# A fused attention and expert kernel: the three-part split of k and q made with TensorE subtractions, the routing work and the squares dealt out anew

## What is computed

```python
q = (x @ Wq.T + bq).reshape(B, L, 16, 8);  k, v likewise        # B = 8 sequences of L = 512 rows, 128 wide
p = einsum('blhd,dm->blhm', q, proj) / sqrt(8)                 # 128 angles for each row and head
q_prime = concat([cos(p), sin(p)]) / sqrt(128);  k_prime likewise
kv = einsum('blhm,blhd->bhmd', k_prime, v);  out = einsum('blhm,bhmd->blhd', q_prime, kv)
x = layernorm(x + out @ Wo.T + bo)
# a mixture of 8 experts (128 -> 512 -> 128, relu), the 2 with the largest logits of x @ Wr + br for each row
x = layernorm(x + sum over the two of weight * expert(x))
```

## Time and profile before

| | before |
|---|---|
| median of three runs | 553.1 us (549.98 to 554.34) |
| profiled execution, its own time | 551.36 us |
| its span, first to last instruction | 549.6 us |
| busy: TensorE matmul, VectorE, ScalarE, GpSimd | 88%, 78%, 69%, 75% |
| mean granted TensorE clock | 0.959 of full speed |

### The profile page before, as it was taken

How to read it: one execution, slowest core, us unless ns; L and a number is a source line. 1 busy time by engine, 2 the same in 40 slices (tenths; PEclk the granted TensorE clock), 3 DMA queues, 4 the chain that set the end, 5 groups by cost and what they waited for, 6 DMA issues and landing times.

```text
span 549.6 us, 13153 instructions
## 1 busy us (share of the span) xinstructions
PE 483.9 (88%) x4205; PEld 297.4 (54%) x4205; DVE 427.8 (78%) x907; ACT 381.0 (69%) x533; POOL 410.7 (75%) x474
## 2 busy tenths in 40 slices
PE   6698889999999999999999989689999679999914
PEld 3333344444444444444344444158999678999802
DVE  6769978988988988988988888568677475777654
ACT  2686669789789789789789689376555244565325
POOL 2279549879879889879879889857677656777645
PEclk9899989999999999999999999799999789999957
DMA  4675504705704705604605400032222123222174
GB/s 96 169 228 160 127 1 138 195 16 144 203 20 126 206 17 144 190 16 141 153 15 136 126 17 1 8 84 58 69 65 71 59 75 94 70 65 70 39 273 191
DMA packets 44447, 56.03 MB, mean 102 GB/s; under 512 B 8779, under 2 KB 31541, under 8 KB 44381
## 3 DMA queue, kind: packets, MB, share of 16 engines
q1 hardware_dynamic: 39493, 45.86, 30.5%
q0 software_dynamic: 4320, 8.95, 5.0%
q10 hardware_dynamic: 568, 0.38, 0.2%
HBM read 37.22 MB, written 17.94 MB: 100 GB/s over the span
## 4 chain that ended last, share of the span: by engine, by line
PE 55%; POOL 12%; DVE 12%; issue 9%; ACT 6%; DMA 2%; another core or an unknown queue 2%; SPq 1%; DVEq 0%; ACTq 0%; POOLq 0%
PE ang L786 11%; PE ang L795 10%; PE misc L603 7%; PE ang L583 5%; PE misc L638 5%; DVE turns L1067 5%; DVE feats L1075 4%; POOL feats L1430 3%; PE ang L574 3%; PE ang L570 3%; POOL routed_dram L1561 2%; PE misc L512 2%; PE misc L649 2%; ACT rows_s L893 2%
## 5 line engine op out<-in xcount | busy, mean ns | idle before, releaser
L1067 DVE TENSOR_SCALAR turns<-ang 128x1024 f16<-128x1024 f32 x128 | 155.4, 1217 | 46.4 <-PE ang L574 23.4
L873 ACT ACTIVATE feats<-ang 128x1024 f32<-128x1024 f32 x128 | 131.7, 1029 | 63.6 <-PE ang L583 61.1
L1430 POOL TENSOR_TENSOR feats<-feats 128x1024 f32<-128x1024 f32 x56 | 107.0, 1910 | 48.8 <-ACT feats L874 48.4
L874 ACT ACTIVATE feats<-ang 128x1024 f32<-128x1024 f32 x128 | 131.5, 1028 | 0.0
L1075 DVE TENSOR_TENSOR feats<-feats 128x1024 f32<-128x1024 f32 x72 | 102.5, 1423 | 0.7 <-ACT feats L874 0.6
L1591 POOL DMA_INDIRECT expert_dram<-feats x71 | 69.7, 981 | 36.3 <-DVE feats L1354 28.5
L1561 POOL DMA_INDIRECT routed_dram<-rows_s,slots x64 | 76.3, 1193 | 20.7 <-issue 18.3
L583 PE MATMUL ang<-turns,negi 128*128 128x512 f16 x256 | 77.9, 386 | 12.4 <-DVE turns L1067 10.5
L795 PE MATMUL ang<-experts,feats 128*128 x568 | 77.6, 281 | 5.5 <-DVE feats L1314 5.4
L786 PE MATMUL ang<-feats 128*128 128x128 f32 x568 | 78.1, 282 | 4.5 <-DVE feats L1306 2.2
L944 ACT ACTIVATE feats<-experts 128x644 f32 x71 | 52.5, 739 | 36.8 <-DVE feats L1354 25.3
(11 more groups left out here) (195 smaller groups left out, 597.2 us busy)
## 6 DMA issues: line engine op xcount, KB each, us to landing
stk<-parts_dram SPq DMA_DIRECT2D x189, 96.0 KB
parts_dram<-parts SPq DMA_DIRECT2D x16, 384.0 KB, 3.6
feats<-routed_dram SPq DMA_DIRECT2D x72, 65.5 KB
feats<-expert_dram SPq DMA_DIRECT2D x16, 256.0 KB, 5.4
x_all<-attn_x SPq DMA_DIRECT2D x8, 256.0 KB, 4.8
experts<-ffn_W SPq DMA_DIRECT2D x8, 256.0 KB
out<-feats SPq DMA_DIRECT2D x8, 256.0 KB, 2.2
x_in<-attn_x SPq DMA_DIRECT2D x7, 256.0 KB
```

The costliest lines, as they stand in the source:

```text
L873: act.activation(f[:, 0, :], a, ACT.Sin, scale=TWO_PI)
L874: act.activation(f[:, 1, :], a, ACT.Sin, scale=TWO_PI / 2).then_inc(s["sines"], 1)
L1067: dve.tensor_scalar(turns[:, u % 2, :], ang[:, slot(ph, u), :], MAGIC, -MAGIC, ALU.add, ALU.add)\
L1430: pool.tensor_tensor(f, f, f, ALU.mult).then_inc(s["sq_p"], 1)
```

## The change

For batches 1 to 7 the split no longer goes through `qk_f` and GpSimd. ScalarE reads the projection in PSUM and writes part 0; TensorE adds minus part 0 to the same PSUM bank (`part_off`, a matmul with a negative identity in bf16, `negb`); ScalarE reads the bank again for part 1; TensorE subtracts that; ScalarE reads part 2. The factor `TURN` goes into the weights. k's projection moves from unit 6 to unit 2 and to the first bank of `misc`, its subtractions stand in units 3 and 4; q's projection stands in unit 6, its subtractions in 7 and 8. Since k's parts are in the bank that kv products write, kv's first step waits for them and moves from unit 4 to 5, where the second stands too. The one-hot rows are made on VectorE by one comparison each. `POOL_SQ` has eight units (2, 3, 4, 6, 7, 8, 10, 12) instead of seven (1, 3, 4, 6, 8, 10, 12). Row transposes, logits, the routing pieces and the ranks each move one unit later, and the ranks go to the last quarter of the first bank of `misc`, behind the first two out products.

```diff
-KV_STEP = [4, 5, 6, 7, 8, 9, 10, 11]
-KV_LAST = [5, 5, 6, 7, 8, 9, 10, 11]
+KV_STEP = [5, 5, 6, 7, 8, 9, 10, 11]
-POOL_SQ = (1, 3, 4, 6, 8, 10, 12)
+POOL_SQ = (2, 3, 4, 6, 7, 8, 10, 12)
...
+            def part_off(b, side, i):
+                pe.wait_ge(s["neg_ok"], 1)
+                wait(pe, "kq"[side] + "_ev", 3, b, i - 1)
+                pe.matmul(misc[:, side, :], negb[:, :], parts[:, side, i, :], start=False, stop=True,
+                          skip_group_check=True).then_inc(s["kq"[side] + "_off"], 1)
...
-                    for step in (k for k, at in enumerate(KV_LAST if last else KV_STEP) if at == u):
-                        kv_product(b, step, *(("raw_ev", 1, b, 3) if first else ("bp_ev", 1, 0, 2) if last
-                                                             else ("xT_ev", 1, b, 2)))
+                    for step in (k for k, at in enumerate(KV_STEP) if at == u):
+                        kv_product(b, step, *(("bp_ev", 1, 0, 2) if last else ("k_ev", 3, b, 4)))
                     if u == 4 and not first:
                         wo_product(b - 1)
+                    if u == 2 and not last:
+                        project(0, 0, b + 1, "xT_ev", 1, b, 2)
+                    if u in (3, 4) and not last:
+                        part_off(b + 1, 0, u - 3)
                     if u == 6 and not last:
-                        project(0, 1, b + 1, *(("v_ev", 1, b, 1) if first else ("y_ok", 1, b, 0)))
-                    if u == 7 and not last:
-                        project(1, 1, b + 1, "k_ev", 1, b, 2)
-                    if u == 8 and not first:
-                        rows_T(b - 1, *(("b2_ok", 1, 0, 2) if last else ("q_ev", 1, b, 2)))
+                        project(1, 1, b + 1, *(("raw_ev", 1, b, 3) if first else ("y_ok", 1, b, 0)))
+                    if u in (7, 8) and not last:
+                        part_off(b + 1, 1, u - 7)
                     if u == 9 and not first:
+                        rows_T(b - 1, *(("b2_ok", 1, 0, 2) if last else ("q_ev", 3, b, 4)))
+                    if u == 10 and not first:
                         logits(b - 1, "xr_ev", 1, b, 0)
                     if u == 12:
                         kv_turn(b)
+                    if u == 13:
+                        out_product(b, 0, 0, *(("q_ev", 3, b, 4) if first else ("lg_ok", 1, b, 0)))
+                        out_product(b, 0, 1)
                         if not first:
-                            ranks(b - 1, "lg_ok", 1, b, 0)
-                    if u == 13:
-                        out_product(b, 0, 0, *(("q_ev", 1, b, 2) if first else ("based", 1, b, 0)))
-                        out_product(b, 0, 1)
+                            ranks(b - 1, "kv_ev", 1, b, 1)
                     if u == 14:
-                        c_product(b)
+                        c_product(b, "based", 1, b, 0)
...
+            def part_evac(b, side, i):
+                if i == 0:
+                    wait(act, "kq"[side] + "_mm", 1, b, 1)
+                    wait(act, "parts_out", 32, b, 16 * side - 16)
...
+                else:
+                    wait(act, "kq"[side] + "_off", 2, b, i - 2)
+                act.activation(parts[:, side, i, :], misc[:, side, :], ACT.Identity, bias=bqk_t[:, side:side + 1])\
+                    .then_inc(s["kq"[side] + "_ev"], 1)
...
-                    if u in (6, 7) and not last:
-                        proj_evac(b + 1, u - 6, 1)
-                    if u == 8 and not first:
+                    if u in (2, 3, 4) and not last:
+                        part_evac(b + 1, 0, u - 2)
+                    if u in (6, 7, 8) and not last:
+                        part_evac(b + 1, 1, u - 6)
+                    if u == 9 and not first:
                         rows_evac(b - 1)
...
-            BEFORE_ROUND = ((6, moments), (10, take_logits), (13, move_base))
-            AFTER_ROUND = ((5, residual), (10, largest))
-            AFTER_SQUARE = ((5, statistics), (10, which), (12, take_ranks), (13, slot_numbers))
+            BEFORE_ROUND = ((6, moments), (11, take_logits), (14, move_base))
+            AFTER_ROUND = ((5, residual), (11, largest), (12, one_hot))
+            AFTER_SQUARE = ((5, statistics), (11, which), (13, take_ranks), (14, slot_numbers))
...
-                    if u in (7, 9) and not last:
-                        split(pool, b + 1, (u - 7) // 2)
...
-                    if u == 11 and not first:
+                    if u == 12 and not first:
                         chosen(b - 1)
-                    if u == 13 and not first:
+                    if u == 14 and not first:
                         slots_of_picks(b - 1)
-                    if u in (14, 15) and not first:
-                        send_rows(b - 1, u - 14)
+                    if u == 15 and not first:
+                        for k in range(TOPK):
+                            send_rows(b - 1, k)
```

More of the change, by code:

```diff
@@ L383, in write @@
                 def write(side):
-                    hold(sp, "split", 6, b, 3 * side + 3)
+                    if b:
+                        wait(sp, "kq"[side] + "_ev", 3, b, 1)
+                    else:
+                        sp.wait_ge(s["split"], 3 * side + 3)
                     dst = parts_dram[b, side].rearrange("i r n -> r i n")
@@ L619, in kv_turn, with c_product @@
                 mm.then_inc(s["kv_mm"], 1)
-            def c_product(b):
+            def c_product(b, *free):
                 wait(pe, "kv_ev", 1, b, 1)
+                wait(pe, *free)
                 pe.matmul(misc[:, 0, 2 * P:2 * P + 2], kv_c[:, :], minus_half[:, :], start=True, stop=True)\
@@ L851, in out_evac, with proj_evac @@
                 act.activation(outT[:, :], misc[:, 1, :], ACT.Identity, bias=c_sum[:, :]).then_inc(s["out_ev"], 1)
-            def proj_evac(b, side, bank):
-                wait(act, "kq"[side] + "_mm", 1, b, 1)
-                wait(act, "split", 6, b, 3 * side - 3)
-                wait(act, "parts_out", 32, b, 16 * side - 16)
-                act.activation(parts[:, side, 0, :], misc[:, bank, :], ACT.Identity,
-                               bias=bqk_t[:, side:side + 1], scale=TURN)
-                act.activation(qk_f[:, side, :], misc[:, bank, :], ACT.Identity,
-                               bias=bqk_t[:, side:side + 1], scale=TURN).then_inc(s["kq"[side] + "_ev"], 1)
+            def proj_evac(side, bank):
+                act.wait_ge(s["kq"[side] + "_mm"], 1)
+                act.activation(parts[:, side, 0, :], misc[:, bank, :], ACT.Identity, bias=bqk_t[:, side:side + 1])
+                act.activation(qk_f[:, side, :], misc[:, bank, :], ACT.Identity,
+                               bias=bqk_t[:, side:side + 1]).then_inc(s["kq"[side] + "_ev"], 1)
+            def part_evac(b, side, i):
+                if i == 0:
+                    wait(act, "kq"[side] + "_mm", 1, b, 1)
+                    wait(act, "parts_out", 32, b, 16 * side - 16)
+                    if b == 1:
+                        wait(act, "split", 3, side, 3)
+                else:
+                    wait(act, "kq"[side] + "_off", 2, b, i - 2)
+                act.activation(parts[:, side, i, :], misc[:, side, :], ACT.Identity, bias=bqk_t[:, side:side + 1])\
+                    .then_inc(s["kq"[side] + "_ev"], 1)
             def sines(b, ph, u):
@@ L1133, in which, with one_hot @@
                 ins.then_inc(s["idx_ok"], 1)
+            def one_hot(b):
+                hold(dve, "idx_ok", 1, b, 1)
+                for k in range(TOPK):
+                    ins = dve.tensor_tensor(hot[:, k, :, :], over(iota[:, :].unsqueeze(1), tile8),
+                                            over(idx8[:, :, k:k + 1], tile8), ALU.is_equal)
+                ins.then_inc(s["hot_ok"], 1)
             n_picks = LT * EXP
@@ L1296, in _ @@
             square(e, -1)
-            LAST_PIECES = ((1, residual), (2, statistics), (3, moments), (16, take_logits), (17, largest), (18, which),
+            LAST_PIECES = ((1, residual), (2, statistics), (3, moments), (16, take_logits), (17, largest), (18, which), (19, one_hot),
                            (23, take_ranks), (24, move_base), (26, slot_numbers))
@@ L1450, in early_counts @@
             def early_counts():
-                pool.wait_ge(s["split"], 6 * BATCH)
+                pool.wait_ge(s["split"], 6)
                 pool.wait_ge(s["based"], EARLY_BATCHES)
@@ L1522, in body @@
                         add_bo(pool, BATCH - 1)
[L1523 removed]
+                    if u == 12 and not first:
                         chosen(b - 1)
[L1525 removed]
+                    if u == 14 and not first:
                         slots_of_picks(b - 1)
[L1527 to L1528 removed]
+                    if u == 15 and not first:
+                        for k in range(TOPK):
+                            send_rows(b - 1, k)
             def chosen(b):
                 hold(pool, "idx_ok", 1, b, 1)
[L1533 to L1540 removed]
```

(4 more changed lines are left out.)

45 lines of the change are left out of this document (18 added, 27 removed).

## The result

The changed kernel takes 558.1 us, median of 4 runs (556.9 to 559.7), against 552.2 for the kernel before, run beside it: ratio 1.011, interval 1.006 to 1.016. The forecast was 571 (558 to 585), so the time lies at the lower edge of that range. The direction was right, the size was not: +5.9 us against +19. In every ratio here, slow executions, over 1.5% above the fastest of the same kernel, are left out (two of the four of b_squares are such).

The account below looks back on a forecast made before the run. TensorE was taken to bound the kernel: per batch work +1.1 us and waits 5.0 against 2.1 make +4.0, +20 over batches 2 to 6. With -1 in the last batch that is +19, forecast 571 us (558 to 585).

Parts of the forecast that it names:

- TensorE's own work: Four added 128x512 bf16 matmuls per batch, with the change of weights, cost 0.9 to 1.1 us; 1.1 was counted.
- A sine pair 1.97: ScalarE's time for one pair of sine instructions, 1.97 us, used to walk the chain of parts.
- Wo: In unit 4 TensorE's Wo product waits 0.7 us for outT from ScalarE.
- q's subtraction: In unit 8 TensorE waits 1.2 us for q's part 1, behind the four normalizations in ScalarE's queue.
- kv(0): In unit 5 the first kv product waits 0.9 us for k's part 2, which stands behind sines(3) on ScalarE.
- Unit 11: Top-8, index search and square(9) now follow kvT on VectorE, so TensorE waits 1.1 us ahead of turn(12).
- Out(0,0): The first out product waits 0.6 us (0.2 to 1.0), as one-hot rows stand ahead of kv_c and kv_pad on VectorE.
- I count batch 1 at nothing: Batch 1 nets zero: its old loss from a slow VectorE square and lower clock goes, about as large as the new one.
- The softer chain: Rival: half of the new waits go, leaving +1.5 to 2 us per batch, 561 us; chance 0.12.
- GpSimd first: Rival: GpSimd's square(10) starts ahead of VectorE's square(9), 1.9 us more ahead of turn(12), 581 us; chance 0.09.
- the lower clock: Rival: the new TensorE waits bring 1.2 GHz, about 1.7 us per batch in five or six, 580 us; chance 0.10.
- The fourth rival: Faster, 546 us, if q's part 1 and k's part 2 end earlier and VectorE has 1.1 us less in unit 11; chance 0.07.

Follow-up runs that it names:

- b_squares: Kernel before with only the changed kernel's list of squares on GpSimd; no ratio, four executions between 558.0 and 568.9 us.
- e1: Changed kernel with q's part 1 read ahead of the four normalizations in ScalarE's unit 7; ratio 1.017 to the kernel before.
- e10: Changed kernel with square 9 instead of 8 on GpSimd and the one-hot rows moved ahead of rounding 13; ratio 1.005 to the kernel before.
- e2: Changed kernel with GpSimd taking square 9 and VectorE square 8; ratio 1.009 to the kernel before.
- a_old_squares: Changed kernel with the kernel before's list of squares on GpSimd; ratio 1.015 to the kernel before.
- e4: Changed kernel with the index search ahead of square 9 in VectorE's unit 11; ratio 1.044 to the kernel before.
- e5: Changed kernel with q's parts 1 and 2 both read in ScalarE's unit 7, around the normalizations and ahead of the sines; ratio 1.016.
- e11: Changed kernel, q and k part 2 earlier, square 9 for 8 on GpSimd, one-hot rows later, rows copy, outT and normalizations on VectorE; ratio 0.988.
- e8: Changed kernel, q and k part 2 earlier, square 9 for 8 on GpSimd, one-hot rows later, rows copy on VectorE; ratio 1.000.

## Why the prediction was wrong in size

**A middle batch: +4.0 forecast, +2.4 measured.** This is the step that failed: the mechanism stood (a chain of parts between ScalarE and TensorE, and VectorE's unit 11), but its price was 1.6 us a batch too high, 8.9 of the 13.4 us by which +19 missed +5.6. TensorE's own work accounts for 0.5 of the 1.6, the waits for 1.0, in these terms.
- *TensorE's own work, +1.1.* It is +0.6. The four subtractions were rightly 0.9, but two kv products back to back take 1.87 and not 2 x 1.0, and from kv_turn to the next angles it is 0.89 (222.06 to 222.95) instead of 1.02, since the ranks no longer follow there.
- *"A sine pair 1.97", from the distance in the earlier trace rows.* In that place TensorE set the pace. The pair's own occupancy is 1.82; the trace of the kernel before has 1.80 where the angles were ready (203.96 to 205.76). So the ScalarE walk, four pairs long, came out late: Wo 0.7 forecast and 0.47 measured, q's subtraction 1.2 and 1.10, rows_T 0.3 and 0.23; kv(0) was 0.9 and 0.88. The reason given for the 1.2, the normalizations ahead of part 1, does not carry it: with part 1 ahead of them (e1) the same time is lost before rows_T.
- *Unit 11.* 1.1 forecast, 1.04 measured: right, and e10 and e2 confirm that it is order.
- *Out(0,0), 0.6.* 0.26. Two one-hot rows take 0.23 from start to start (0.25 taken); the 0.3 added for GpSimd's square running beside them was not paid.
- *Turn(0), 0.2.* Nothing.

Waits of 3.98 against 5.0, old ones 2.18 against 2.1. Over batches 2 to 6 this is 12.0 instead of 20 (11.1 on the first chip, where batches 5 and 6 of the kernel before and batch 2 of the changed one were 0.8 to 0.9 longer than on the second).

**"I count batch 1 at nothing", and batch 0 at 0.** The old loss and a new one of 4.0 were set against each other. The old loss was taken rightly (45.1 against 41.05) and it goes; the new one is 2.4, and batch 1 becomes a middle batch of 43.6: -1.5. Batch 0 was credited nothing for the split that leaves GpSimd, though it was named; it gains 1.2 to 2.9, of which 1.2 to 1.3 can be put down to the change and the rest goes with the clock of its first units. In the kernel before, the split's instructions delay a GpSimd square of that batch until it is just ahead of VectorE's. The reason given for batch 1 (square(1) leaves GpSimd) is sufficient in the kernel before (b_squares) and not needed in the changed one (a_old_squares): there VectorE comes 0.08 us ahead of GpSimd instead of 0.07 behind it. What brings it forward was not tested.

**The rest.** The last batch was put at -1, within 2, and measured -0.63 and +1.5, the second half a microsecond outside and not explained. The expert stage was put at 0; -2.6 on one chip and -0.7 on the other, both within what two profiles of nearly the same kernel differ by (3.6). Taken together, +19 becomes +5.6 (spans of the first chip) or +8.5.

**The rivals.** The softer chain was the nearest at 561, for a reason close to it: the pairs are shorter. Its size (+1.5 to 2 a batch) is under the measured 2.4. GpSimd first and the lower clock did not come, and e4 shows both as described when the order is forced. The fourth rival asked for three things at once and had 546. The runs show that its conditions can't all be had by order, since parts taken earlier push the sines (e5). Moving load comes near: a middle batch of e11 is 0.5 under the kernel before, where the rival had 1.0, and e11 is 1.2% under it in all, mostly by batches 0 and 1.

## What to carry to other kernels

When an engine's neighbours are all 87% busy, a step moved from one to another is paid where the receiver is densest, not in its sum: VectorE and GpSimd were relieved of 7.5 us a batch and TensorE waited longer for ScalarE and for VectorE's order of work in one unit. If a reordering makes one wait vanish and an equal one appear behind it, as with e1, that stretch is short of time on the receiving engine: move load off it. Where an engine has slack and only its order is bad, as in VectorE's unit 11, ordering pays; here order gave back 1.7 us of the 2.4 a batch, and load another 1.2. And in costing an edit, take an instruction's spacing from a place where its input was ready, and cost the first iterations by themselves, since there the queues are filled differently.

## What the runs showed of the hardware

- A VectorE square (128x1024, f32) beside GpSimd's: first 1.21 to 1.22, second, by as little as 0.07 us, 2.90; second by 0.31, 2.66. The first to start keeps its time in each of these pairs, and the second takes about what the first has left plus its own time (1.82 and 1.21 for the 2.90). The Trainium skill, SBUF — State Buffer, Who interferes with whom, counts a VectorE instruction with two SBUF inputs beside a GpSimd one that reads SBUF as a contending pair, and says that issue order decides who blocks; every pair here agrees.
- Waits of TensorE of up to 1.24 us, several to a batch, left the granted clock at 1.00 (2.4 GHz) in the middle batches of e1; one of 2.47 us a batch (e4) brought spells at 1.2 GHz in four batches of six, in which eight records of the out product take 1.94 us instead of 1.06. The length of one wait does not settle it: in batch 2 of e8 two waits of 1.21 and 1.39, 2.0 us apart, are followed by 0.82 over ten microseconds, and batch 3 of the same run has a lone 1.39 at 1.00.
- A single bf16 matmul of 128x512 between matmuls of other weights costs 0.21 to 0.23 us from start to start, though its record is 0.38 to 0.39 long.
